# Softmax denominators from pairwise-added key blocks, score tiles between shifted-score pairs, and an unrolled feed-forward stage in an adaLN transformer layer

## What is computed

```python
mod = (silu(c) @ wmod).reshape(4, 6, 1, 512)        # sa, ca, ga, sb, cb, gb
h = layernorm(x) * (1 + ca) + sa
q, k, v = heads of layernorm(h; qn) @ Wq + bq and layernorm(h; kvn) @ Wkv + bkv
q, k = layernorm_per_head(rotary(q * 32**-0.25, h)), the same for k
w = softmax(where(causal, q @ k.T / sqrt(32), min))
x = x + ga * ((w @ v) @ Wo + bo)
h = layernorm(x) * (1 + cb) + sb
x = x + gb * ((silu(h @ w_gate.T) * (h @ w_up.T)) @ w_down.T)
```

## Time and profile before

| | us |
|---|---|
| median of 3 runs | 2522.72 (2519.64 to 2523.82) |
| the profiled execution, its own time | 2521.72 |
| its span, first to last instruction | 2519.8 |
| PE busy | 2316.9 (92%) |
| DVE, ACT, POOL busy | 1170.1, 792.5, 743.2 |

### The profile page before, as it was taken

How to read it: one execution, slowest core, us unless ns; L and a number is a source line. 1 busy time by engine, 2 the same in 40 slices (tenths; PEclk the granted TensorE clock), 3 DMA queues, 4 the chain that set the end, 5 groups by cost and what they waited for, 6 DMA issues and landing times. The chain is left out here.

```text
span 2519.8 us, 33443 instructions
## 1 busy us (share of the span) xinstructions
PE 2316.9 (92%) x12520; PEld 1706.0 (68%) x12520; DVE 1170.1 (46%) x1799; ACT 792.5 (31%) x1671; POOL 743.2 (29%) x823
## 2 busy tenths in 40 slices
PE   6999992899999999999858799999999999999998
PEld 4777771656655665665446587887878787878787
DVE  5999984655555555555269612212121213121212
ACT  3333331244454554454435411111111111111111
POOL 2667773011111111111167222222222222222221
PEclk8999995699999999999989899999999999999999
DMA  6122224643554365443179521212121211212111
GB/s 218 68 100 100 100 92 122 140 101 99 129 135 111 96 144 127 103 99 81 36 248 299 196 68 34 84 34 83 33 80 36 65 51 46 71 46 71 44 56 33
DMA packets 162369, 244.24 MB, mean 97 GB/s; under 512 B 17188, under 2 KB 84356, under 8 KB 161760
## 3 DMA queue, kind: packets, MB, share of 16 engines
q1 hardware_dynamic: 153760, 221.71, 30.2%
q0 software_dynamic: 7456, 18.07, 2.6%
q10 hardware_dynamic: 1056, 3.15, 0.3%
HBM read 132.74 MB, written 59.26 MB: 76 GB/s over the span
## 5 line engine op out<-in xcount | busy, mean ns | idle before, releaser
L882 DVE TENSOR_REDUCE b_top<-b_psA 128x2 f32<-128x1024 f32 (+3 forms) x384 | 363.3, 957 | 288.8 <-PE b_psA L801 165.1
L949 ACT ACTIVATE b_probT<-b_psB 128x512 f32<-128x512 f32 (+3 forms) x768 | 339.7, 491 | 348.5 <-PE b_psB L825 233.0
L1298 DVE TENSOR_TENSOR f_gu<-f_psU,f_silu 128x512 f32<-128x512 f32 x128 | 88.5, 691 | 749.3 <-PE f_psU L1359 749.3
L822 PE MATMUL b_psB<-b_stack 98*128 98x512 f32 (+3 forms) x768 | 287.5, 413 | 7.1 <-ACT b_probT L949 5.8
L801 PE MATMUL b_psA<-b_stack 96*128 96x512 f32 (+3 forms) x768 | 256.5, 392 | 27.9 <-DMA b_stack<-b_halves 20.2
L822 PEld LDWEIGHTS b_psB<-b_stack 98*128 98x128 f32 x768 | 139.8, 188 | 190.8 <-issue 118.5
L57 POOL TENSOR_TENSOR f_spots<-f_still 1x1 f32<-1x1 f32 x128 | 25.9, 202 | 794.8 <-PE f_psD L1347 788.7
L1288 ACT ACTIVATE f_silu<-f_psG 128x512 f32<-128x512 f32 x128 | 76.6, 598 | 523.5 <-PE f_psG L1359 523.5
L1345 PE MATMUL f_psD<-f_wd_hi,f_gu_hi 128*128 128x512 f32 x512 | 201.1, 393 | 22.8 <-DVE f_gu_lo L1302 12.3
L1357 PE MATMUL f_psG<-f_hT_hi,w_hi 128*128 128x512 f32 x512 | 200.6, 392 | 10.9 <-DVE f_hT_lo L1309 10.9
L1358 PE MATMUL f_psG<-f_hT_hi,w_lo 128*128 128x512 f32 x512 | 199.9, 390 | 0.0
(11 more groups left out here) (179 smaller groups left out, 4210.2 us busy)
## 6 DMA issues: line engine op xcount, KB each, us to landing
b_stack<-b_halves SPq DMA_DIRECT2D x192, 256.0 KB, 5.0
f_wd<-in_wd_t SPq DMA_DIRECT2D x128, 256.0 KB, 2.6
qkv_d<-a_t SPq DMA_DIRECT2D x32, 512.0 KB, 2.7
b_land<-qkv_d SPq DMA_DIRECT2D x32, 512.0 KB, 4.6
a_x<-in_x SPq DMA_DIRECT2D x32, 256.0 KB, 3.3
qkv_d<-a_v SPq DMA_DIRECT2D x32, 256.0 KB, 3.0
b_v<-qkv_d SPq DMA_DIRECT2D x16, 512.0 KB, 5.9
att_d<-b_att SPq DMA_DIRECT2D x16, 512.0 KB, 3.2
```

What stands on the lines that cost most here:

```text
L822: mm = pe.matmul(psB[:, i % 2, cols], stack[0:NR, n % BUFS, 0, j, kb * P:(kb + 1) * P], stack[0:NR, n % BUFS, 1, j, first * P:(half + 1) * ...
L882: dve.tensor_reduce(out, slot("score", NI * n + i)[:, :, 0:width], AX.X, ALU.max, negate=True).then_inc(s["maxed"], 1)
L949: act.activation(probT[:, (NW * n + w) % 3, j, 0:width], psB[:, i % 2, 0:width], ACT.Exp).then_inc(s["expd"], 1)
```

## The change

- **Pairs of key blocks.** POOL adds the exponentials of key block 2i + 1 to those of block 2i, head by head (`add_pair`, four adds), after the product with v has read block 2i. PE makes one product with ones per pair (`add_up`), three steps after the pair's last shift. `b_probT` has five buffers, not three. ACT copies `b_psL` two steps later than before.
- **Order of a step.** PE: shift 0, shift 1, both score tiles, shift 2, shift 3. DVE copies `b_psO` before the reductions of its step.
- **Denominators.** The seven DMAs by way of DRAM move from POOL's queue to SP's, in steps 6, 7, 9 and 10. DVE's reciprocal stays in step 8, POOL's product goes to step 11, the store of the result to step 2 of the next unit.
- **Feed-forward.** No loops: 128 chunks in one list. h has two buffers and is split in chunks 8 to 11 of the block before; every `down` lags two chunks; `scale` starts with each quarter of the last `down` and `add` comes one chunk later; x1 lies where h landed; POOL's small pause is gone.

```diff
@@ -589,6 +589,7 @@
     assert NI == 2 * NW
     SHIFT_LAG = NW + 2
     BUFS = 3
+    PROBS = 5
...
+    def pair_at(k):
+        at = shift_at(k)
+        return (at[0], at[1] // 2) if at and at[1] % 2 == 1 else None
+
+    def sum_at(k):
+        return pair_at(k - 3)
+
     def take_at(k):
         at = shift_at(k - 2)
         return (at[0], BLOCKS[at[1]][0]) if at and BLOCKS[at[1]][1] == (BLOCKS[at[1]][0] + 1) * HALF - 1 else None
+
+    def take_sum_at(k):
+        return take_at(k - 2)
...
-        probT = sb("b_probT", [P, 3, 4, W])
+        probT = sb("b_probT", [P, PROBS, 4, W])
...
+            def sums_out(n):
+                sp.wait_ge(s["taken_l"], 2 * n + 2)
+                sp.dma_start(scratch["sums"][0], sums[0:P:HD, n % 2]).then_inc(s["sums_out"], 16)
+
+            def few_in(n):
+                sp.wait_ge(s["sums_out"], 16 * n + 16)
+                sp.dma_start(few[:, 0], scratch["sums"][0].rearrange("j (a c) -> (j a) c", c=C // HD)).then_inc(s["few_in"], 16)
+
+            def few_out(n):
+                sp.wait_ge(s["inverted"], n + 1)
+                sp.dma_start(scratch["sums"][1].rearrange("j (a c) -> (j a) c", c=C // HD), few[:, 1]).then_inc(s["few_out"], 16)
+
+            def wide_in(n):
+                sp.wait_ge(s["few_out"], 16 * n + 16)
+                for j in range(4):
+                    sp.dma_start(sums[j * HD:(j + 1) * HD, n % 2], scratch["sums"][1, j:j + 1].broadcast_to([HD, C])).then_inc(s["wide_in"], 16)
...
-                if w == 10 and 0 <= n - 2 < NG:
-                    store(n - 2)
+                if 0 <= n - 2 < NG - 1:
+                    if w == 6:
+                        sums_out(n - 2)
+                    if w == 7:
+                        few_in(n - 2)
+                    if w == 9:
+                        few_out(n - 2)
+                    if w == 10:
+                        wide_in(n - 2)
+                if w == 2 and 0 <= n - 3 < NG:
+                    store(n - 3)
...
+            def add_pair(n, i):
+                half, kb = BLOCKS[2 * i + 1]
+                width = (half + 1) * W - max(kb, half * HALF) * P
+                at = (NW * n + 2 * i) % PROBS
+                whole_at = (half + 1) * W - max(kb - 1, half * HALF) * P
+                pool.wait_ge(s["weighed"], NW * n + 2 * i + 1)
+                for j in range(4):
+                    into = probT[:, at, j, whole_at - width:whole_at]
+                    pool.wait_ge(s["expd"], 4 * (NW * n + 2 * i + 1) + j + 1)
+                    add = pool.tensor_tensor(into, into, probT[:, (at + 1) % PROBS, j, 0:width], ALU.add)
+                add.then_inc(s["added"], 1)
+
             def normalise(n):
-                pool.wait_ge(s["taken_l"], 2 * n + 2)
-                pool.dma_start(scratch["sums"][0], sums[0:P:HD, n % 2]).then_inc(s["sums_out"], 16)
-                pool.wait_ge(s["sums_out"], 16 * n + 16)
-                pool.dma_start(few[:, 0], scratch["sums"][0].rearrange("j (a c) -> (j a) c", c=C // HD)).then_inc(s["few_in"], 16)
-                pool.wait_ge(s["inverted"], n + 1)
-                pool.dma_start(scratch["sums"][1].rearrange("j (a c) -> (j a) c", c=C // HD), few[:, 1]).then_inc(s["few_out"], 16)
-                pool.wait_ge(s["few_out"], 16 * n + 16)
-                for j in range(4):
-                    pool.dma_start(sums[j * HD:(j + 1) * HD, n % 2], scratch["sums"][1, j:j + 1].broadcast_to([HD, C])).then_inc(s["wide_in"], 16)
                 pool.wait_ge(s["wide_in"], 64 * n + 64)
                 pool.wait_ge(s["taken_o"], 2 * n + 2)
                 pool.tensor_tensor(att[:, n % 2], att[:, n % 2], sums[:, n % 2], ALU.mult).then_inc(s["scaled"], 1)
@@ -769,9 +809,11 @@
             for k in STEPS:
                 if prep_at(k):
                     high(*prep_at(k))
-                at = take_at(k)
-                if at and at[1] == 1 and at[0] < NG - 1:
-                    normalise(at[0])
+                if pair_at(k):
+                    add_pair(*pair_at(k))
+                n, w = unit(k)
+                if w == 11 and 0 <= n - 2 < NG - 1:
+                    normalise(n - 2)
...
-            def weigh(n, w, summing):
+            def weigh(n, w):
                 half, kb = BLOCKS[w]
-                if not summing:
-                    pe.wait_ge(s["expd"], 4 * (NW * n + w) + 4)
-                    if w == 0:
-                        pe.wait_ge(s["v_in"], 16 * n + 16)
+                pe.wait_ge(s["expd"], 4 * (NW * n + w) + 4)
+                if w == 0:
+                    pe.wait_ge(s["v_in"], 16 * n + 16)
                 if kb == 0:
-                    at_least(pe, s["taken_l" if summing else "taken_o"], 2 * n + half)
+                    at_least(pe, s["taken_o"], 2 * n + half)
                 first = max(kb, half * HALF)
-                out = psL if summing else psO
                 for j in range(4):
                     rows = slice(j * HD, (j + 1) * HD)
-                    mm = pe.matmul(out[rows, (first - half * HALF) * P:W], ones[:] if summing else v[:, n % 2, kb, rows],
-                                   probT[:, (NW * n + w) % 3, j, 0:(half + 1) * W - first * P],
+                    mm = pe.matmul(psO[rows, (first - half * HALF) * P:W], v[:, n % 2, kb, rows],
+                                   probT[:, (NW * n + w) % PROBS, j, 0:(half + 1) * W - first * P],
                                    start=(kb == 0), stop=(kb == (half + 1) * HALF - 1), skip_group_check=True)
-                mm.then_inc(s["summed" if summing else "weighed"], 1)
+                mm.then_inc(s["weighed"], 1)
+
+            def add_up(n, i):
+                half, kb = BLOCKS[2 * i]
+                pe.wait_ge(s["added"], NW // 2 * n + i + 1)
+                if kb == 0:
+                    at_least(pe, s["taken_l"], 2 * n + half)
+                first = max(kb, half * HALF)
+                for j in range(4):
+                    mm = pe.matmul(psL[j * HD:(j + 1) * HD, (first - half * HALF) * P:W], ones[:],
+                                   probT[:, (NW * n + 2 * i) % PROBS, j, 0:(half + 1) * W - first * P],
+                                   start=(kb == 0), stop=(kb == (half + 1) * HALF - 2), skip_group_check=True)
+                mm.then_inc(s["summed"], 1)
 
             for k in STEPS:
                 for i in range(2):
                     if shift_at(k):
                         shift(*shift_at(k), 2 * i)
                         shift(*shift_at(k), 2 * i + 1)
-                    if score_at(k):
+                    if i == 0 and score_at(k):
                         n, w = score_at(k)
-                        score(n, 2 * w + i)
+                        score(n, 2 * w)
+                        score(n, 2 * w + 1)
                 if prep_at(k):
                     prepare(*prep_at(k))
                 if peaks_at(k) is not None:
                     turn_peaks(peaks_at(k))
                 if weigh_at(k):
-                    weigh(*weigh_at(k), False)
-                    weigh(*weigh_at(k), True)
+                    weigh(*weigh_at(k))
+                if sum_at(k):
+                    add_up(*sum_at(k))
...
             for k in STEPS:
+                if take_at(k):
+                    take(*take_at(k))
                 for i in range(2):
                     if score_at(k):
                         n, w = score_at(k)
                         peak(n, 2 * w + i)
-                    if i == 0 and take_at(k):
-                        take(*take_at(k))
                 if score_at(k) and score_at(k)[1] == NW - 1:
                     gather(score_at(k)[0])
                 if prep_at(k):
                     low(*prep_at(k))
-                at = take_at(k - 5)
-                if at and at[1] == 1 and at[0] < NG - 1:
-                    dve.wait_ge(s["few_in"], 16 * at[0] + 16)
+                n, w = unit(k)
+                if w == 8 and 0 <= n - 2 < NG - 1:
+                    dve.wait_ge(s["few_in"], 16 * (n - 2) + 16)
                     dve.reciprocal(few[:, 1], few[:, 0]).then_inc(s["inverted"], 1)
-                at = take_at(k)
+                at = take_sum_at(k)
                 if at and at[0] == NG - 1:
                     finish(at[1])
...
-                    at_least(act, s["summed"], NW * n + w - 2)
-                    at_least(act, s["weighed"], NW * n + w - 2)
+                    before = NW * n + w - PROBS
+                    if before % 2 == 0:
+                        at_least(act, s["summed"], before // 2 + 1)
+                    else:
+                        at_least(act, s["added"], before // 2 + 1)
+                        at_least(act, s["weighed"], before + 1)
                 width = (half + 1) * W - max(kb, half * HALF) * P
-                act.activation(probT[:, (NW * n + w) % 3, j, 0:width], psB[:, i % 2, 0:width], ACT.Exp).then_inc(s["expd"], 1)
+                act.activation(probT[:, (NW * n + w) % PROBS, j, 0:width], psB[:, i % 2, 0:width], ACT.Exp).then_inc(s["expd"], 1)
...
 ```

(124 more changed lines are left out.)

128 lines of the change are left out of this document (46 added, 82 removed).

## The result

| | before | after |
|---|---|---|
| median, us | 2522.09 (2519.64 to 2523.82, 4 runs) | 2556.74 (2555.74 to 2560.74, 4 runs) |
| ratio to before | | 1.0141, interval 1.0124 to 1.0159 |
| profiled span, us | 2519.8 | 2553.9 |
| unit of attention, us | 49.40 | 54.6 |
| feed-forward, first product to end, us | 1083.2 | 1052.7 |

The change made the kernel 1.4% slower; the forecast was 2511. Feed-forward gained the 30.5 us that were expected of it. Attention lost 60: the last product with v ends at 1315.0 instead of 1254.9.

A forecast was written before the change was run, and what follows sets the result against it. PE was taken to set the pace in attention, busy 48.84 of 49.40 us a unit, with waits hidden inside. 2521.7 + 34 (stalled units) - 14 (other units) - 30.4 (feed-forward) = 2511 us, range 2445 to 2550.

The forecast's parts named there:

- POOL's adds: In attention, POOL stays below 32 of 44 us a unit, so adds cost nothing; 1.3 us taken for 512 columns.
- The rival with POOL at twice the price: In attention, adds of 2.6 us for 512 columns make `add_up` wait, POOL at 49 us a unit, around 2520; chance 0.03.
- the step for the unstalled unit: An attention unit where nothing else waits takes 49.4 - 3.6 - 3.2 + 1.2 = 43.8 us, 5.6 less.
- The DMAs that change queue: From S, first transfer of `lay_stacks`: `few_in` queues behind stacks, lands S + 22; DVE waits some 10 us, 13 times.
- The end S + 17.1: Other end for `sums_out` landing in SP's queue, against S + 19.8 taken; overtaking makes a unit 2.7 us shorter, the whole 35.
- The stalled unit: Attention units 2 to 14 take 24.3 + 26.3 = 50.6 us, 52.0 with the clock, 2.6 more than before: +34 us.
- The clock: After PE's pause of about 6 us in a stalled unit, 3.4 us at half speed cost 1.4 us, between 0 and 3.
- The order: PE's new shift order in attention gains 3.2 us a unit, between 2 and 4; late reductions in steps 3, 5 cost 1.2.
- the ones product: In attention, one product with ones per pair of key blocks instead of per block: net gain 3.6 us a unit.
- feed-forward: Seven block boundaries without waits, with the first's half clock, give 28.4 us, the stage's end 2.0: together -30.4.
- the stall costs more than all gains: In attention, small transfers each need 1 us more and the clock falls for 6 us: unit 55.6, total 2558; chance 0.27.
- No stall: In attention step 8, `sums_out` passes the stacks or SP's issue is not held: 2404; chance with half a stall 0.2.

The follow-up runs named there:

- Experiment 9: The changed kernel with POOL's adds waiting until DVE's `low` of that step or `gather` is over, nothing else: 2505.5 us, 0.9944 of the kernel before.
- experiment 5: The changed kernel with the reciprocal moved to step 11, its followers later, and POOL's adds waiting for DVE's `low` or `gather`: 2408.4 us, 0.9552 of the kernel before.
- 6: The changed kernel with the reciprocal in step 11, its followers later, and POOL's adds cut to one column, so denominators are incomplete: 2407.0 us, 0.9546 of the kernel before.
- experiment 1: The changed kernel with DVE's reciprocal moved from step 8 to 11 and the transfers and product behind it moved later: 2467.9 us, 0.9783 of the kernel before.
- 2: The changed kernel with the seven small transfers issued on ACT's queue instead of SP's: 2501.0 us, 0.9916 of the kernel before.
- experiment 10: The kernel of Experiment 9 plus 20 unused products keeping PE busy in the stall, units 2 to 14: 2475.4 us, 0.9829 of the kernel before.
- experiment 7: The kernel before with only PE's new order of a step and DVE's early copy of `b_psO`: 2488.6 us, 0.9870 of the kernel before.
- experiment 4: The kernel before with the new feed-forward stage alone: 2492.5 us, 0.9879 of the kernel before.

## Why the prediction was wrong

**POOL's adds: the step that failed.** "So the adds cost nothing, as long as one of 512 columns takes under 2.5 us." The duration was right, 1.28, and PE waited for POOL only once, 1.75 us in front of the last product with ones. But the step asked only whether POOL has time, not what an add does to DVE. Experiment 9 gives the price of that, 51 us, where the prediction had 0: 13 units by 3.4, and 7 in unit 1. With the adds apart the changed kernel takes 2505.5; the forecast was 2511. The miss is 46 us, and this term is more than the whole of it; the other terms together were 5.5 us too pessimistic. The rival with POOL at twice the price looked at the wrong engine. In the step for the unstalled unit the forecast of 43.8 is right (44.05, experiments 5 and 6) only with the adds apart; with them it was 46.8 in the kernel after (54.6 less the 7.8 that step 10 has over its 4.40).

**The DMAs that change queue: right.** Issue at S + 19.8 and reduction at S + 24.3 were met within 0.1, the landing within 0.4, the count is 13, and experiments 1 and 2 remove it in two ways. The end S + 17.1, the small transfer that overtakes, was not what happened.

**The stalled unit: right in sum, with its parts off.** Forecast 50.6 without the clock; experiment 10 shows 49.2. The rest of the loop, 26.3 in the forecast and 24.8 measured (49.2 less 24.4), was put too long, above all by the 1.2 for late reductions: experiment 7 shows 0.25 in step 3 and nothing in step 5, in its unit of 47.24.

**The clock: right that it falls, its size off.** Each pause of some 5 us was followed by 6.8 us at 0.50, twice the 3.4 that were taken. It cost 2.0 us a unit (10 against 9), not 1.4, 8 us in all. The fall in unit 1 had no place in the sum.

**The order, the ones product, feed-forward: right in size.** Experiment 7 shows 2.16 for the order against 2.0, but this sum was right by luck: 2.4 gained and 0.25 lost, not 3.2 and 1.2. From 7 to 5 the unit falls by another 3.19, against 3.6 for the ones product. Feed-forward: 30.5 in the trace and 29.8 in experiment 4, against 30.4.

**The rivals.** The time of "the stall costs more than all gains", 2558, was met, but mostly by another cause: of its mechanism, the longer fall of the clock came (6.8 us; it had 6), worth 0.6 us a unit more than forecast, and the small transfers that need 1 us more each did not. Of its 6.2 us a unit (49.4 to 55.6), 5.2 were seen; 3.4 of these were the adds, which also turned unit 1 from a gain of 5.3 (experiment 9) into a loss of 1.9. "No stall", 2404, is what experiment 5 then reached: 2408.

What stays open: how the early copy and the pair of score tiles share the 2.16 of experiment 7, and how much of the 3.4 a unit would be left if only one of the two added waits of experiment 5 were set.

## What to carry to other kernels

Before work goes to an idle engine, look in the trace for operations of the neighbour that are longer there than elsewhere with the same shape: busy time that grows with an unchanged count and unchanged shapes can be a held engine, and here no wait list showed it. Price a moved transfer by the queue it will stand in and by when its reader comes: the same move cost 12 us of the whole in units of 49.4 us, and 5.1 us in each of 13 units (7 with the clock) once the unit was shorter. And when a change is a bundle, the loss can sometimes be taken back by small moves in the right place: here two `wait_ge` on POOL and a reciprocal three steps later, with the transfers behind it, turned +1.4% into -4.5%.

## What the runs showed of the hardware that was not expected

- A pause of PE of 5.1 us was followed by 6.8 us at 0.50 in each of 13 units. The clock also fell without such a pause, behind several shorter waits: for 10.2 us in unit 1 of the kernel after, where PE had been busy 5.31 of the 6.5 us before (5.96 of the same 6.5 us in experiment 9, where it stayed at 1.00), and for some 3.4 us in about every other unit of experiment 1, where PE had been busy 3.79 of 5.4 us before one of these falls. When PE was kept busy over the pause and nothing else held it, the clock stayed at 1.00 for 757.8 us.
- GpSimd adds held VectorE operations that read SBUF: three operations of 0.19 us took 0.93 us each beside adds of 1.00. An operation of 1.23 us also held an add, four of which took 4.86 us instead of 3.87. VectorE operations that read PSUM were not held (0.95 both ways).
- 16 KB behind 512 KB in one queue had landed 0.2 us after it; on SP's queue 16 KB read after that took 1.8 us, on ACT's queue beside the stacks 4.4.
